# Softmax and head division over two banks of PSUM per operation, in a six-layer local-attention kernel

## The chip, the cores and the metric

The kernel runs on one core of one Trainium2 chip. The metric is the device time of one execution in microseconds. Five engines work side by side, each through its own queue in order: TensorE (PE) does matrix products and transposes, VectorE (DVE) and ScalarE (ACT) do elementwise work and reductions, GpSimd (POOL) does elementwise work on data in SBUF, and SyncE (SP) issues the transfers. They wait for each other on semaphores.

## The reference, cut to what matters

One time-mixing layer with a norm comes first, then six layers of local attention and a gated feed-forward over 2048 tokens of width 128, then a last norm. What the change touches is in the attention, with 16 heads of 64 and windows of 32 tokens that see themselves and the window before:

```
sim = jnp.einsum('bhwie,bhwje->bhwij', bq, bk2) * QK_SCALE
sim = jnp.where(mask, -jnp.finfo(sim.dtype).max, sim)
attn = jax.nn.softmax(sim, -1)
out = jnp.einsum('bhwij,bhwje->bhwie', attn, bv2)
...
for i in range(DEPTH):
    x = attn_layer(shift_tokens(x), Wqkv[i], q_scale[i], k_scale[i], Wo[i]) + x
    x = ffn_layer(shift_tokens(x), ln_g[i], ln_b[i], W1[i], b1[i], W2[i], b2[i]) + x
```

The feed-forward of a layer is a norm over the width, a product up to twice 341, a gelu on one half times the other, and a product down.

## The kernel before

The tokens are 16 tiles of 128, so six layers are 96 tiles in a row. The function `layers` runs steps s = -1 to 99. A step works on several tiles at once, each in a different phase: tile s + 1 is projected ("p": queries, keys, their squares, the inverse root of the sums, the unit vectors, the values), tile s has its queries and keys transposed and its scores made ("a"), tile s - 1 is mixed with the values, divided and sent through the output matrix ("b"). The feed-forward takes two tiles together: in an odd step the centred input and its variance ("norm") and the product down of an earlier pair ("down"), in an even step the normed input and the products up ("up"). Steps -1 to 6 and 95 to 99 are written out, 7 to 94 are a loop over pairs of an odd and an even step.

The order of the work on each engine is the order in which the functions are written. There is no scheduler. An engine that waits holds up all that is behind it in its queue.

PSUM holds four buffers of two banks, `proj_a`, `proj_b`, `att` and `turn` (in the functions `bank_a`, `bank_b`, `bank_s`, `bank_t`). The heads with an even number lie in the first bank, those with an odd number in the second. So each of the scores (in `turn`) and the mixed heads (in `att`) fills two banks, and the kernel before takes them bank by bank:

- `centre_scores(par)` on DVE: the row maxima of one bank (L1053, into `row_max`), then scores minus maximum (L1056, into `logits`).
- `weigh(par)` on ACT: the exponential of one bank (L949, into `probs`).
- `divide_out(par)` on DVE: mixed heads of one bank times the inverse of the mass (L1045, into `heads_out`).

PE makes the scores of both banks in one interleaved run (L1228) and so signals both at its end; the same holds for the mixed heads (L1202).

In an even step two operations of the feed-forward stand between the banks. On DVE `norm_n` (L1102), the centred input times the inverse deviation that PE's L1259 spread over the partitions, is between `centre_scores(0)` and `centre_scores(1)`. On ACT `normed` (L1009), `norm_n` with gain and bias, is between `weigh(0)` and `weigh(1)`. PE's products up (L1152) wait for `normed`, and stand in PE's queue behind the output product (L1265).

The other names that matter: `squares` (ACT L942) and their `sums` (DVE L1039); the inverse root, nine small operations on DVE (L88 to L104); `unit` (DVE L1064), first of the queries, then of the keys; on POOL `across` (L886), `along` (L920), `rotated` (L894), `turns` (L905), the shifted inputs `shift_f` and `shift_a` (L874, L875, L913, L914); PE's transposes (L1135), its query and key projections (L1168, L1183) and its value projection (L1240), which waits for `unit` of the queries.

Of the kernel before, what the change touches and what calls it, by code (L numbers as in the profile page):

```python
# [26 lines left out]
ALU = mybir.AluOpType  # L27
ACT = mybir.ActivationFunctionType
AX = mybir.AxisListType
# [4 lines left out]
HEADS, HEAD = 16, 64  # L34
PAIRS = HEADS // 2
INNER = HEADS * HEAD
DEPTH = 6
WINDOW = 32
# [27 lines left out]
def after(engine, semaphore, count):  # L66

    if not isinstance(count, int) or count > 0:
        engine.wait_ge(semaphore, count)
# [633 lines left out]
def layers(nc, ctx, given):  # L703
# [9 lines left out]
    bank_a, bank_b, bank_s, bank_t = (given[k] for k in ("proj_a", "proj_b", "att", "turn"))  # L713
    passed = given["passed"]

    with ExitStack() as own:
        def sb(name, shape, dtype=F32):
            return own.enter_context(nc.sbuf_tensor(name, shape, dtype))

        def sem(name):  # L720
            return ctx.enter_context(nc.semaphore(name))
# [19 lines left out]
        row_max = sb("row_max", [128, HEADS])  # L741
        logits = sb("logits", [128, 2, PAIRS, 2 * WINDOW])
        probs = sb("probs", [128, PAIRS, 2, 2 * WINDOW])
        mass = sb("mass", [128, HEADS])
        inv_mass = sb("inv_mass", [128, HEADS])
        p_t = sb("p_t", [128, PAIRS, TILE])
        heads_out = sb("heads_out", [128, PAIRS, 2, HEAD])
# [28 lines left out]
        scored, maxed, centred, weighed = sem("scored"), sem("maxed"), sem("centred"), sem("weighed")  # L776
        massed, mass_inverted = sem("massed"), sem("mass_inverted")
        p_turned, p_laid, mixed, scaled_out = sem("p_turned"), sem("p_laid"), sem("mixed"), sem("scaled_out")
# [37 lines left out]
        with nc.Block() as block:  # L816
# [118 lines left out]
            def _(act):  # L935
                def step(s, h, odd, live):
                    p, a, b, mine = s + 1, s, s - 1, 1 - odd
# [4 lines left out]
                        act.activation(squares[j][:, :, :], by_head((bank_a, bank_b)[j]), ACT.Square)\  # L942
                            .then_inc(squared[j], 1)

                    def weigh(par):
                        act.wait_ge(centred, 2 * a + par + 1)
                        after(act, p_turned, 2 * a)
                        after(act, massed, a)
                        act.activation(probs[:, :, par, :], logits[:, par, :, :], ACT.Exp).then_inc(weighed, 1)  # L949

                    if live["down"]:
                        act.wait_ge(down_in, (layer_of(s - 5) + 1) * 32)
# [48 lines left out]
                        act.copy(v_tok[mine][:, :, :, :], bank_a[:, :, :].rearrange("p a (h e) -> p a h e", e=HEAD))\  # L1001
                            .then_inc(v_laid, 1)
                    if live["a"]:
                        weigh(0)
                    if live["up"]:
                        act.wait_ge(scaled_f, h + 2)
                        act.wait_ge(up_in, (layer_of(s - 4) + 1) * 48)
                        after(act, widened, NC_ * (h + 1))
                        act.activation(normed[:, :], norm_n[:, :], ACT.Identity, bias=w_ffn[:, F_B:F_B + 1],  # L1009
                                       scale=w_ffn[:, F_G:F_G + 1]).then_inc(normed_f, 1)  # L1010
                    if live["a"]:
                        weigh(1)
                    if live["norm"]:
                        act.wait_ge(dev_made, h + 2)
                        after(act, scaled_f, h + 1)
# [2 lines left out]
                        act.activation(dev_sq[:, :], bank_b[:, 0, 0:TWO], ACT.Square).then_inc(dev_squared, 1)  # L1018

                run(act, step)  # L1020

            @block.vector
            def _(dve):
# [9 lines left out]
                def step(s, h, odd, live):  # L1033
                    p, a, b, mine = s + 1, s, s - 1, 1 - odd
# [3 lines left out]
                        after(dve, rooted, ROOT_OPS * p)  # L1038
                        dve.tensor_reduce(sums[:, j, :], squares[j][:, :, :], AX.X, ALU.add).then_inc(summed[j], 1)  # L1039

                    def divide_out(par):
                        dve.wait_ge(mixed, 2 * b + par + 1)
                        dve.wait_ge(mass_inverted, b + 1)
                        after(dve, o_turned, 2 * b)
                        dve.tensor_tensor(heads_out[:, :, par, :], bank_s[:, par, :].rearrange("p (a e) -> p a e", e=HEAD),  # L1045
                                          inv_mass[:, :].rearrange("p (a b) -> p a b", b=2)[:, :, par].unsqueeze(2)
                                          .broadcast_to([128, PAIRS, HEAD]), ALU.mult).then_inc(scaled_out, 1)

                    def centre_scores(par):
                        heads = slice(PAIRS * par, PAIRS * par + PAIRS)  # L1050
                        scores = bank_t[:, par, :].rearrange("p (a c) -> p a c", a=PAIRS)
                        dve.wait_ge(scored, 2 * a + par + 1)
                        dve.tensor_reduce(row_max[:, heads], scores, AX.X, ALU.max).then_inc(maxed, 1)  # L1053
                        dve.wait_ge(maxed, 2 * a + par + 1)
                        after(dve, weighed, 2 * a)
                        dve.tensor_tensor(logits[:, par, :, :], scores,  # L1056
                                          row_max[:, heads].unsqueeze(2).broadcast_to([128, PAIRS, 2 * WINDOW]),
                                          ALU.subtract).then_inc(centred, 1)

                    def unite(j):  # L1060
                        dve.wait_ge(rooted, ROOT_OPS * p + ROOT_OPS)
# [22 lines left out]
                        sum_squares(0)  # L1084
                        sum_squares(1)
                    if live["b"]:
                        divide_out(0)
                        divide_out(1)
                    if live["p"]:
                        dve.wait_ge(summed[0], p + 1)  # L1090
                        dve.wait_ge(summed[1], p + 1)
# [3 lines left out]
                        unite(0)  # L1095
                        unite(1)
                    if live["a"]:
                        centre_scores(0)
                    if live["up"]:
                        dve.wait_ge(rstd_spread, h + 2)  # L1100
                        after(dve, normed_f, h + 1)
                        dve.tensor_tensor(norm_n[:, :], dev[:, :], bank_s[:, 1, 0:TWO], ALU.mult).then_inc(scaled_f, 1)  # L1102
                    if live["a"]:
                        centre_scores(1)
                    if live["down"]:
                        dve.wait_ge(narrowed, h + 1)
                        dve.scalar_tensor_tensor(xa[:, columns(s - 5, 2)], bank_b[:, 1, 0:TWO], w_ffn[:, F_B2:F_B2 + 1],
# [10 lines left out]
                    if live["p"]:  # L1118
# [5 lines left out]
                                          ALU.mult).then_inc(alonged[1], 1)  # L1124

                run(dve, step)

            @block.tensor
# [311 lines left out]
```

## Time and profile before

| | |
|---|---|
| median of 3 runs | 2161.71 us (2158.82 to 2162.98) |
| the profiled execution | 2161.64 us |
| its span, first to last instruction | 2159.5 us |
| mean granted TensorE clock over the span | 0.919 |
| granted clock from 400 to 2100 us | 1.00 |
| busy PE, DVE, POOL, ACT | 1890.9, 1694.1, 1457.0, 1170.8 us |

The profile is of one execution. Its page gives the busy time of each engine and the costliest groups of instructions; the trace behind it can be asked for who waited for whom and for the instructions in order of time. PE's rows name matrix products, PEld their weight loads, which overlap the products. Times in the rows are in microseconds from the start of the span.

### The profile page before, as it was taken

The page shows a single profiled execution, that of the slowest core. Times are in us where ns is not written, and L with a number is a line of the kernel's source. Part 1 is how long each engine was busy: PE and PEld are TensorE (multiplying, and loading weights), DVE is VectorE, ACT ScalarE, POOL GpSimd, SP SyncE. Part 2 cuts the span into 40 slices and gives each one's busy share as a digit, 9 for nine tenths or more (in the row PEclk, how much of TensorE's full clock was granted, in tenths as well). Part 3 has the DMA queues.
Part 4 walks back from the last instruction along what each step waited for, and adds up shares of the span by engine and source line. Part 5 has one row for each costly group of instructions (what it writes and reads, how often), then busy time and mean ns, then how long its engine had stood idle before and what let it go on. Part 6 is the DMA issues. An engine that isn't in the chain of part 4 may idle for free. (4 is left out here: it accounts for less than half of the span.)

```text
span 2159.5 us, 87406 instructions
## 1 busy us (share of the span) xinstructions
PE 1890.9 (88%) x34160; PEld 1385.6 (64%) x34160; DVE 1694.1 (78%) x3442; ACT 1170.8 (54%) x2085; POOL 1457.0 (67%) x1150
## 2 busy tenths in 40 slices
PE   6776766899999999999999999999999999999995
PEld 4555543676666666666666676666666666666664
DVE  5777775888888888878788888888888878888874
ACT  1111113566656666666666666666666666656662
POOL 0000005888888887878787888888787878787871
PEclk6555557999999999999999999999999999999997
DMA  4000001222232222322222322223222223222220
GB/s 140 1 0 0 0 0 40 61 61 60 58 88 64 71 56 55 86 65 67 55 57 58 87 72 65 58 58 85 65 66 55 56 56 84 73 62 58 58 59 20
DMA packets 93565, 123.18 MB, mean 57 GB/s; under 512 B 27760, under 2 KB 41808, under 8 KB 93392
## 3 DMA queue, kind: packets, MB, share of 16 engines
q1 hardware_dynamic: 93232, 122.42, 22.5%
q8 instruction: 31, 0.51, 0.1%
q10 hardware_dynamic: 288, 0.13, 0.0%
q14 instruction: 14, 0.11, 0.0%
HBM read 20.74 MB, written 1.05 MB: 10 GB/s over the span
## 5 line engine op out<-in xcount | busy, mean ns | idle before, releaser
L886 POOL TENSOR_TENSOR across<-unit,turns 128x512 f32<-128x512 f32 x384 | 525.2, 1389 | 263.3 <-issue 252.3
L894 POOL TENSOR_TENSOR rotated<-along,across 128x1024 f32<-128x1024 f32 x192 | 496.2, 2584 | 20.4 <-POOL along L920 9.6
L1039 DVE TENSOR_REDUCE sums<-squares 128x16 f32<-128x1024 f32 x192 | 234.1, 1219 | 162.7 <-ACT squares L942 156.7
L1135 PE MATMUL turn<-identity,rotated 128*128 128x128 f32 x1536 | 204.2, 276 | 53.5 <-POOL rotated L894 53.5
L1135 PEld LDWEIGHTS turn<-identity,rotated 128*128 128x128 f32 x1536 | 172.1, 141 | 116.0 <-issue 101.1
L920 POOL TENSOR_TENSOR along<-unit,turns 128x1024 f32<-128x1024 f32 x96 | 227.6, 2371 | 0.0
L1240 PE MATMUL proj_a<-w_qkv,shift_a 128*128 128x512 f32 x384 | 189.5, 616 | 35.1 <-DVE unit L1064 25.4
L1001 ACT COPY val<-proj_a 128x1024 f32<-128x1024 f32 x96 | 97.2, 1012 | 179.6 <-PE proj_a L1240 179.6
L1265 PEld LDWEIGHTS att<-o_t,w_o 128*128 128x128 f32 x1536 | 188.2, 193 | 6.1 <-issue 1.0
L1168 PE MATMUL proj_a<-w_qkv,shift_a 128*128 128x512 f32 x384 | 185.7, 607 | 3.9 <-POOL shift_a L874 2.6
L1265 PE MATMUL att<-o_t,w_o 128*128 128x128 f32 x1536 | 188.6, 276 | 0.0
L977 ACT COPY k_t<-turn 128x512 f32<-128x512 f32 x192 | 103.1, 589 | 151.2 <-PE turn L1135 151.2
L1122 DVE TENSOR_TENSOR along<-unit,turns 128x1024 f32<-128x1024 f32 x96 | 183.6, 1913 | 0.0
L1183 PE MATMUL proj_b<-w_qkv,shift_a 128*128 128x512 f32 x384 | 181.5, 595 | 0.0
L942 ACT ACTIVATE squares<-proj_a 128x1024 f32<-128x1024 f32 x96 | 98.3, 1024 | 116.3 <-PE proj_a L1168 116.3
L1202 PE MATMUL att<-v_win,p_t 64*32 64x64 f32 x12288 | 154.0, 225 | 2.9 <-issue 2.1
L1228 PEld LDWEIGHTS turn<-k_t,q_t 64*32 64x32 f32 x12288 | 128.0, 105 | 41.0 <-issue 40.7
L962 ACT COPY p_t<-att 128x512 f32<-128x512 f32 x192 | 103.0, 589 | 88.9 <-PE att L1135 88.9
L1202 PEld LDWEIGHTS att<-v_win,p_t 64*32 64x32 f32 x12288 | 135.6, 105 | 21.8 <-issue 19.2
L1045 DVE TENSOR_TENSOR heads_out<-att,inv_mass 128x512 f32<-128x512 f32 x192 | 123.6, 686 | 31.9 <-PE att L1202 31.7
L1228 PE MATMUL turn<-k_t,q_t 64*32 64x64 f32 x12288 | 143.9, 225 | 0.0
L1056 DVE TENSOR_TENSOR logits<-turn,row_max 128x512 f32<-128x512 f32 x192 | 132.8, 691 | 6.6
(183 smaller groups left out, 3783.2 us busy)
## 6 DMA issues: line engine op xcount, KB each, us to landing
v_win<-val SPq DMA_DIRECT2D x1536, 64.0 KB
w_qkv<-wqkv_dram SPq DMA_DIRECT2D x18, 512.0 KB, 3.9
w_o<-wo_dram SPq DMA_DIRECT2D x6, 512.0 KB, 4.3
where<-positions_dram SPq DMA_DIRECT2D x1, 2048.0 KB, 10.8
w_ffn<-ffn_dram SPq DMA_DIRECT2D x12, 170.5 KB, 2.3
w_ffn<-ffn_dram SPq DMA_DIRECT2D x6, 192.0 KB, 2.3
x_tok<-x_dram SPq DMA_DIRECT2D x4, 256.0 KB, 4.5
out_dram<-final SPq DMA_DIRECT2D x4, 256.0 KB, 2.4
```

Of the source, the lines that this page charges most:

```text
L886: pool.tensor_tensor(a[:, :, 1 - half, :], u[:, :, half, :], table, ALU.mult)\
L894: pool.tensor_tensor(rotated[j][:, :, :], along[j][:, :, :], across[j][:, :, :], ALU.add).then_inc(rotated_in[j], 1)
L920: pool.tensor_tensor(along[0][:, :, :], unit[0][:, :, :], turns[mine][:, 0, :].unsqueeze(1).broadcast_to([128, HEADS, HEAD]), ALU.mult).th ...
L1039: dve.tensor_reduce(sums[:, j, :], squares[j][:, :, :], AX.X, ALU.add).then_inc(summed[j], 1)
L1122: dve.tensor_tensor(along[1][:, :, :], unit[1][:, :, :], turns[mine][:, 2, :].unsqueeze(1).broadcast_to([128, HEADS, HEAD]), ALU.mult).the ...
L1135: mm = pe.transpose(bank[:, TILE * (i % 4):TILE * (i % 4) + TILE], buffer[:, TILE * i:TILE * i + TILE], identity[:, :])
L1168: mm = pe.matmul(bank_a[:, half, :], shift_a[mine][:, :], w_qkv[:, 512 * half:512 * half + 512], start=True, stop=True)
L1183: mm = pe.matmul(bank_b[:, half, :], shift_a[mine][:, :], w_qkv[:, base:base + 512], start=True, stop=True)
L1202: mm = pe.matmul(bank_s[WINDOW * w:WINDOW * w + WINDOW, par, HEAD * a_:HEAD * a_ + HEAD], p_t[rows, a_, WINDOW * w:WINDOW * w + WINDOW], v ...
L1228: mm = pe.matmul(bank_t[WINDOW * w:WINDOW * w + WINDOW, par, HEAD * a_:HEAD * a_ + HEAD], q_t[rows, a_, WINDOW * w:WINDOW * w + WINDOW], k ...
L1240: pe.matmul(bank_a[:, par, :].rearrange("p (a e) -> p a e", a=PAIRS), shift_a[mine][:, :], values[:, par, :, :], start=True, stop=True).th ...
L1265: mm = pe.matmul(bank_s[:, 0, 0:TILE], w_o[:, a_, :], o_t[:, a_, :], start=(a_ == 0), stop=(a_ == PAIRS - 1))
```

## The change

Each pair of operations becomes one that runs over both banks: maxima, subtraction, exponential and division. The semaphores are counted up by 2 in one go, so that the engines that wait need no change. In the even steps the feed-forward operations that stood between the banks now stand behind the single operations.

```diff
-                    def weigh(par):
-                        act.wait_ge(centred, 2 * a + par + 1)
+                    def weigh():
+                        act.wait_ge(centred, 2 * a + 2)
                         after(act, p_turned, 2 * a)
                         after(act, massed, a)
-                        act.activation(probs[:, :, par, :], logits[:, par, :, :], ACT.Exp).then_inc(weighed, 1)
+                        act.activation(probs[:, :, :, :].rearrange("p a b c -> p b a c"), logits[:, :, :, :], ACT.Exp)\
+                            .then_inc(weighed, 2)
...
                     if live["a"]:
-                        weigh(0)
+                        weigh()
                     if live["up"]:
...
-                    if live["a"]:
-                        weigh(1)
...
-                    def divide_out(par):
-                        dve.wait_ge(mixed, 2 * b + par + 1)
+                    def divide_out():
+                        dve.wait_ge(mixed, 2 * b + 2)
...
-                        dve.tensor_tensor(heads_out[:, :, par, :], bank_s[:, par, :].rearrange("p (a e) -> p a e", e=HEAD),
-                                          inv_mass[:, :].rearrange("p (a b) -> p a b", b=2)[:, :, par].unsqueeze(2)
-                                          .broadcast_to([128, PAIRS, HEAD]), ALU.mult).then_inc(scaled_out, 1)
...
+                        dve.tensor_tensor(heads_out[:, :, :, :].rearrange("p a b e -> p b a e"),
+                                          bank_s[:, :, :].rearrange("p b (a e) -> p b a e", e=HEAD),
+                                          inv_mass[:, :].rearrange("p (a b) -> p b a", b=2).unsqueeze(3)
+                                          .broadcast_to([128, 2, PAIRS, HEAD]), ALU.mult).then_inc(scaled_out, 2)
+
+                    def centre_scores():
+                        scores = bank_t[:, :, :].rearrange("p b (a c) -> p (b a) c", c=2 * WINDOW)
+                        dve.wait_ge(scored, 2 * a + 2)
+                        dve.tensor_reduce(row_max[:, :], scores, AX.X, ALU.max).then_inc(maxed, 2)
+                        dve.wait_ge(maxed, 2 * a + 2)
                         after(dve, weighed, 2 * a)
...
+                        dve.tensor_tensor(logits[:, :, :, :].rearrange("p b a c -> p (b a) c"), scores,
+                                          row_max[:, :].unsqueeze(2).broadcast_to([128, HEADS, 2 * WINDOW]),
+                                          ALU.subtract).then_inc(centred, 2)
...
                     if live["a"]:
-                        centre_scores(0)
+                        centre_scores()
                     if live["up"]:
                         dve.wait_ge(rstd_spread, h + 2)
                         after(dve, normed_f, h + 1)
                         dve.tensor_tensor(norm_n[:, :], dev[:, :], bank_s[:, 1, 0:TWO], ALU.mult).then_inc(scaled_f, 1)
-                    if live["a"]:
-                        centre_scores(1)
```

On DVE, at the end of an even step (step 6), the queue reads before:

```order
L1064 TENSOR_TENSOR unit<-proj_b,inv_norm 128x1024 [waits k_acrossed,k_alonged,rooted]
L1053 TENSOR_REDUCE row_max<-turn 128x8 [waits scored]
L1056 TENSOR_TENSOR logits<-turn,row_max 128x512 [waits weighed,maxed]
L1102 TENSOR_TENSOR norm_n<-dev,att 128x256 [waits normed_f,rstd_spread]
L1053 TENSOR_REDUCE row_max<-turn 128x8 [waits scored]
L1056 TENSOR_TENSOR logits<-turn,row_max 128x512 [waits weighed,maxed]
L1111 TENSOR_TENSOR xb<-att,xa 128x128 [waits attended]
```

and now:

```order
L1063 TENSOR_TENSOR unit<-proj_b,inv_norm 128x1024 [waits k_acrossed,k_alonged,rooted]
L1052 TENSOR_REDUCE row_max<-turn 128x16 [waits scored]
L1055 TENSOR_TENSOR logits<-turn,row_max 128x1024 [waits weighed,maxed]
L1100 TENSOR_TENSOR norm_n<-dev,att 128x256 [waits normed_f,rstd_spread]
L1107 TENSOR_TENSOR xb<-att,xa 128x128 [waits attended]
```

`norm_n` has both banks of scores ahead of it in place of one.

On ACT, at the end of the same even step, the queue reads before:

```order
L992 COPY o_t<-att 128x512 [waits attended,o_turned] x2
L996 ACTIVATE k_t<-k_t,carry_scale 128x8x32 [waits scored]
L1001 COPY val<-proj_a 128x1024 [waits v_spread,v_projected]
L949 ACTIVATE probs<-logits 128x8x64 [waits massed,p_turned,centred]
L1009 ACTIVATE normed<-norm_n,w_ffn 128x256 [waits widened,up_in,scaled_f]
L949 ACTIVATE probs<-logits 128x8x64 [waits massed,p_turned,centred]
```

and now:

```order
L993 COPY o_t<-att 128x512 [waits attended,o_turned] x2
L997 ACTIVATE k_t<-k_t,carry_scale 128x8x32 [waits scored]
L1002 COPY val<-proj_a 128x1024 [waits v_spread,v_projected]
L949 ACTIVATE probs<-logits 128x2x8x64 [waits p_turned,massed,centred]
L1010 ACTIVATE normed<-norm_n,w_ffn 128x256 [waits widened,up_in,scaled_f]
```

`normed` now has the whole exponential ahead of it, and that waits for the whole subtraction.

## Rows read from the trace of the kernel before

**Rows 1.** The page's first part: busy us (share of span) x instructions, by engine.
```profile
PE 1890.9 (88%) x34160; PEld 1385.6 (64%) x34160; DVE 1694.1 (78%) x3442; ACT 1170.8 (54%) x2085; POOL 1457.0 (67%) x1150
```
**Rows 2.** Who waited for whom: us in total, times, longest us.
```profile
DVE sums L1039 <- ACT squares L942: 156.7, 146, 7.5
...
ACT squares L942 <- PE proj_a L1168: 116.3, 96, 6.1
...
PE turn L1135 <- POOL rotated L894: 53.5, 51, 2.2
...
PE att L1135 <- DVE heads_out L1045: 24.0, 47, 1.3
...
PEld proj_b L1152 <- ACT normed L1009: 7.5, 44, 0.2
```
**Rows 3.** Timeline, end of an even step: start us, us, engine, line, operation [idle before <-releaser].
```profile
1019.99 0.68 DVE L1053 TENSOR_REDUCE row_max<-turn 128x8 f32<-128x512 f32 x1
...
1020.84 0.59 PE L1259 MATMUL att<-rstd_diag,ones 128*128 128x256 f32 x2
...
1021.27 1.95 PE L1265 MATMUL att<-o_t,w_o 128*128 128x128 f32 x16
1021.47 0.42 DVE L1102 TENSOR_TENSOR norm_n<-dev,att 128x256 f32<-128x256 f32 x1
...
1021.80 0.69 DVE L1053 TENSOR_REDUCE row_max<-turn 128x8 f32<-128x512 f32 x1
1022.02 0.63 ACT L949 ACTIVATE probs<-logits 128x512 f32<-128x512 f32 x1
...
1022.52 0.69 DVE L1056 TENSOR_TENSOR logits<-turn,row_max 128x512 f32<-128x512 f32 x1
1022.55 0.59 ACT L1009 ACTIVATE normed<-norm_n,w_ffn 128x256 f32<-128x256 f32 x1
...
1023.20 1.99 PE L1152 MATMUL proj_b<-normed,w_ffn 128*128 128x256 f32 x8
```
**Rows 4.** Timeline, the odd step after it, from the division of the heads.
```profile
1032.95 1.29 DVE L1045 TENSOR_TENSOR heads_out<-att,inv_mass 128x512 f32<-128x512 f32 x2 [0.28 <-PE att L1202]
...
1034.54 0.29 POOL L874 COPY shift_a<-xa 64x128 f32 x1 [0.38 <-POOL shift_f L914]
1034.60 0.27 DVE L92 TENSOR_TENSOR root_work<-inv_norm 128x32 f32<-128x32 f32 x1
1034.88 0.29 POOL L875 COPY shift_a<-xa 64x128 f32 x1
1034.90 0.32 DVE L94 TENSOR_TENSOR root_work<-root_work,sums_min 128x32 f32<-128x32 f32 x1
...
1035.93 0.19 DVE L102 TENSOR_TENSOR root_work<-root_work,sums_min 128x32 f32<-128x32 f32 x1
...
1037.80 0.67 PE L1240 MATMUL proj_a<-w_qkv,shift_a 128*128 128x512 f32 x1 [0.57 <-DVE unit L1064]
...
1037.84 1.27 POOL L886 TENSOR_TENSOR across<-unit,turns 128x512 f32<-128x512 f32 x1 [2.66 <-issue]
```
**Rows 5.** Durations: one line's (ns min/median/max), then groups of the page (mean ns).
```profile
L1064 DVE TENSOR_TENSOR unit<-proj_a,inv_norm x96: 1223/1225/1226, 341.6 to 2086.4; 128x1024 f32<-128x1024 f32 x96
...
L1039 DVE TENSOR_REDUCE sums<-squares 128x16 f32<-128x1024 f32 x192 | 234.1, 1219 | 162.7 <-ACT squares L942 156.7
...
L1001 ACT COPY val<-proj_a 128x1024 f32<-128x1024 f32 x96 | 97.2, 1012 | 179.6 <-PE proj_a L1240 179.6
...
L992 ACT COPY o_t<-att 128x512 f32<-128x512 f32 x192 | 102.3, 587 | 6.7 <-PE att L1135 6.7
```
**Rows 6.** Timeline: POOL's last product and PE's transposes of it, even step, then odd.
```profile
1014.92 1.09 PE L1135 MATMUL turn<-identity,rotated 128*128 128x128 f32 x8 [1.00 <-POOL rotated L894]
...
1029.78 2.38 POOL L894 TENSOR_TENSOR rotated<-along,across 128x1024 f32<-128x1024 f32 x1
...
1032.66 1.09 PE L1135 MATMUL turn<-identity,rotated 128*128 128x128 f32 x8
```

More of the change, by code:

```diff
@@ L1049, in centre_scores @@
[L1049 to L1054, printed above, removed]
+                        dve.tensor_tensor(heads_out[:, :, :, :].rearrange("p a b e -> p b a e"),
+                                          bank_s[:, :, :].rearrange("p b (a e) -> p b a e", e=HEAD),
+                                          inv_mass[:, :].rearrange("p (a b) -> p b a", b=2).unsqueeze(3)
+                                          .broadcast_to([128, 2, PAIRS, HEAD]), ALU.mult).then_inc(scaled_out, 2)
@@ L1055, in centre_scores @@
+                    def centre_scores():
[3 more added lines that the diff above has]
+                        dve.wait_ge(maxed, 2 * a + 2)
                         after(dve, weighed, 2 * a)
-                        dve.tensor_tensor(logits[:, par, :, :], scores,
-                                          row_max[:, heads].unsqueeze(2).broadcast_to([128, PAIRS, 2 * WINDOW]),
-                                          ALU.subtract).then_inc(centred, 1)
+                        dve.tensor_tensor(logits[:, :, :, :].rearrange("p b a c -> p (b a) c"), scores,
+                                          row_max[:, :].unsqueeze(2).broadcast_to([128, HEADS, 2 * WINDOW]),
+                                          ALU.subtract).then_inc(centred, 2)
@@ L1086, in step @@
                     if live["b"]:
-                        divide_out(0)
-                        divide_out(1)
+                        divide_out()
                     if live["p"]:
```

## The prediction

> **What bounds the kernel now.** The layers' first `unit` starts at 341.6 us [rows 5], and they fill the rest but for the last norm. Their 96 steps repeat in pairs, an odd step and an even one. Which end is last inside such a pair has to be read from the order of time, since no engine is full: the page gives PE 88% of the span and DVE 78% [rows 1]. I read first who waited for whom, and then one pair in the timeline.
>
> The waits [rows 2] show PE as the engine that rarely stops. It stops in the even steps for the last product of the rotation on POOL (53.5 us, 51 times), and in the odd steps for the divided heads on DVE (24.0 us, 47 times). Its weight loads stop 44 times for `normed`, but only for 7.5 us in all. DVE in contrast waits for ACT's squares for 156.7 us, and those squares wait for a projection on PE. So DVE is mostly behind PE and not ahead of it, and a microsecond saved on DVE is worth something only in front of an instruction for which PE, or the POOL chain, is waiting.
>
> The even step's end [rows 3]: PE runs the 1.95 us of L1265 from 1021.27 to 1023.22 and goes on at 1023.20 with L1152, which needs `normed`. `normed` ran on ACT from 1022.55 to 1023.14. There is **no slack**: `normed` is finished when PE is. It comes from `norm_n` on DVE, which ran at 1021.47, straight after the first bank's subtraction and as soon as PE's L1259 (1020.84 + 0.59 = 1021.43) had its operand. The second bank's maximum and subtraction came after it, at 1021.80 and 1022.52.
>
> The odd step [rows 4]: once PE has the heads mixed, DVE divides both banks (1.29 us for two operations that overlap a little), runs the nine small operations of the inverse root, and makes the unit vectors, for which PE then waits 0.57 us at L1240 (1037.80). The POOL chain that the next even step waits for begins there as well. Two of the small operations, L92 and L94, took 0.27 and 0.32 us where L102, the same kind and size, took 0.19; in that stretch POOL copies `shift_a` (1034.54 to 1035.17).
>
> The even step's stall for POOL is 1.00 us at 1014.92, and in the odd step POOL had its `rotated` at 1029.78 + 2.38 = 1032.16, 0.50 us before PE took it at 1032.66 [rows 6].
>
> **The change, part by part.** First the durations. A DVE product from PSUM over both banks is already in the trace: `unit` 128x1024 takes 1.225 us. A reduce of 1024 takes 1.219. On ACT a 1024-wide copy takes 1.012 and a 512-wide copy 0.587, so 512 more elements cost 0.425; the exponential of one bank takes 0.63, and both in one 1.06 [rows 3, 5]. The ends for the exponential: 1.02, as the 1024-wide squares or copy take, and 1.26, twice the 0.63. For the DVE operations: 1.22 and 1.37 (twice 0.69). I take the low ones for DVE, since a row of just that form has them.
>
> (a) Maximum and subtraction in the **odd** steps. Four operations of 0.68 or 0.69, 2.74 us, become two of 1.22 with a gap of 0.03 (as 1021.80 + 0.69 to 1022.52 [rows 3]), 2.47. What comes next on DVE there is the feed-forward residual `xa` and then `xb`, which waits for PE's L1265, and PE asks for the probabilities only in its next step. Worth nothing.
>
> (b) The same in the **even** steps, where `norm_n` stood between the banks. Now it is behind both. The maximum runs 1019.99 to 1021.21, the subtraction from 1021.24 to 1022.46, and `norm_n` after that, not at 1021.47. Nor can ACT start `normed` at once, since the exponential of both banks is ahead of it in ACT's queue: it waits for the whole subtraction (the first bank's waited only for a quarter of the work), runs 1022.49 to 1023.55, and `normed` starts about 0.10 before that ends, as it did before (1022.55 against 1022.65): 1023.45. Before: 1022.55. That is **+0.90 us**, and PE had no slack [rows 3]. `norm_n` itself is done by 1022.9 and so is not the last. PE stands still for some 0.9 us in front of L1152.
>
> (c) What the delay carries along. In the odd step that follows everything on PE queues behind L1152, and ACT, then DVE, wait for PE there [rows 2]. Only POOL is not delayed. In an odd step it had 0.50 us to spare, now it has more, so it takes back nothing. The even step's 1.00 us of waiting for POOL can't absorb it either: that POOL chain starts from `unit` of the odd step, behind the delay. So the +0.90 enters whole.
>
> (d) `heads_out` in one operation: 1.29 becomes 1.22, **-0.07 us** in front of the root in the odd step, on the path. In the even step PE waits for POOL then, and it is worth nothing.
>
> (e) A side effect: POOL's copies of `shift_a` stay where they are, while DVE's L92 and L94 come 0.83 later, at about 1035.43, after their end at 1035.17 [rows 4]. If the overlap was what made them long, both fall to 0.19: (0.27 - 0.19) + (0.32 - 0.19) = **-0.21 us** on the path. Bounds: 0 and -0.21. I take it whole, for every other small operation of the chain that met no POOL work took 0.19.
> The Trainium skill (SBUF — State Buffer, "Who interferes with whom") says that a DVE instruction with two SBUF inputs contends with a GpSimd instruction that reads SBUF; by this rule the gain of (e) is real, and by a reading in which the overlap is chance the sum would be 9.7 us longer. The trace agrees so far: L92 and L94 have two such inputs, and were long just there.
>
> Sum: there are 46 even steps that have both attention and the up-projection (steps 4 to 94). 46 x (0.90 - 0.07 - 0.21) = 46 x 0.62 = **+28.5 us**. The profiled execution took 2161.64 (span 2159.5), which is the median of the runs as well (2161.71). Forecast: 2161.6 + 28.5 = **2190 us**.
>
> **The rivals.**
> *No relief on the small operations.* As forecast, but (e) is 0: 46 x 0.83 = 38, so 2200 us. For it: L92 and L94 may be long for a reason that moves with them. Chance 0.17.
> *The wide operations cost twice the narrow ones.* Each bank of PSUM might be worked off as its own pass: maximum 1.36, subtraction 1.38, exponential 1.26. Then `normed` starts 1019.99 + 1.36 + 0.03 + 1.38 + 0.03 + 1.26 - 0.10 = 1023.95, 1.40 us late; the divide costs 0.08 more (twice 0.69 against 1.29); 46 x (1.40 + 0.08 - 0.21) = 58, so 2220 us. The rows of 1024 elements speak against it. Chance 0.05.
> *POOL is the clock of the pair.* If the POOL chain ran free of PE, PE's 1.00 us wait in the even step would shrink by the 0.90 and no more would be seen: 2158 to 2162 us, no change. It decides if the POOL chain starts before the delayed work. Against it: it starts with `unit`, and the engine idles 2.66 us before that [rows 4]. Chance 0.06.
> *DVE is the bound after all.* Then every step saves what DVE saves: 2.74 - 2.47 = 0.27 for the scores and 0.07 for the heads, 0.34 x 96 = 33 us: 2129 us, faster. For it: DVE works in the pair as much as any but PE. Against it: it is idle before the sums of the squares, 146 times in 192 [rows 2]. Half such a saving, where (b) turns out to be covered, ends near 2145. The point from which it decides: PE would need 0.90 us of slack in front of L1152, and it has none. Chance 0.07.
> The Trainium skill (VectorE: DVE Perf Modes, "The TRN2 errata") speaks for this rival: a fixed latency is paid per instruction, so fewer and larger tiles are to be preferred. The trace agrees on the fixed part (two of 0.69 against one of 1.225), but here it is paid where nobody waits.
> *The change does not do what it says* can be left out: the order of instructions shows the single wide operations.
>
> **How the numbers follow.** Forecast 0.65, no relief 0.17, twice as dear 0.05, POOL clock 0.06, DVE bound 0.07. Low end: in (b) the exponential at 1.02 and 0.2 us more absorbed per pair by some wait that I did not see, 46 x (0.62 - 0.04 - 0.20) = 17, rounded down to 2177. High end: no relief and the exponential at 1.26, 46 x (0.90 + 0.20 - 0.07) = 47: 2209, rounded up to 2210. These ends hold the first two cases, some 0.8. Faster by over 0.2% (what a measurement of this kernel can tell from no change): 0.07. Within 0.2%: 0.06. Slower: 0.87.
>
> **What would show it.** In the profile after: `norm_n` starts just behind the wide subtraction; `normed` some 0.9 us later relative to L1265's start (1.28 us behind it before, 2.2 after); PE idle before L1152 for about 0.9 us in 46 steps, released by ACT `normed`, some 40 us in all; L92 and L94 shorter on average; PE's wait for POOL in the even step still near 1.0; a pair some 0.62 us longer. It would be wrong if PE's wait in front of L1152 were small, if the wait for POOL shrank by what the other grew, or if the wide exponential took far from 1.06.

## The result

The changed kernel takes 2197.07 us (median of 4 runs, 2194.91 to 2198.16) against 2162.35 us before (median of 4 runs): slower, ratio 1.0163 with a 95% interval of 1.0145 to 1.018. That is 34.7 us more, where 28.5 had been forecast. The profiled execution's span is 2196.4 us, 36.9 more than before. Two executions below ran at a lower granted clock, 2426.44 us (0.73) among the ten of e1 and 2659.06 us (0.634) among the fifteen of the kernel before beside e1 to e4: the medians count them, the ratios leave them out.

The first part of the page and the group of the products up, of the changed kernel. The columns are those of [rows 1] and of the page's groups (busy us, mean ns | idle before, releaser):

```profile
PE 1891.4 (86%) x34160; PEld 1385.2 (63%) x34160; DVE 1663.8 (76%) x3154; ACT 1165.8 (53%) x1989; POOL 1455.2 (66%) x1150
...
L1148 PE MATMUL proj_b<-normed,w_ffn 128*128 128x256 f32 x384 | 97.6, 398 | 45.8 <-ACT normed L1010 45.8
```

DVE works 30 us less (1663.8 against 1694.1) and ACT 5 us less, and the kernel is 35 us longer. PE does the same work. What is new is in the last row: PE now stands 45.8 us in front of L1148 (L1152 before), all of it for `normed`. The waits answer to [rows 2]:

```profile
DVE sums L1038 <- ACT squares L942: 181.4, 152, 5.6
...
ACT squares L942 <- PE proj_a L1164: 114.4, 96, 6.1
...
PE turn L1131 <- POOL rotated L894: 53.7, 50, 3.8
...
PEld proj_b L1148 <- ACT normed L1010: 53.1, 45, 1.2
PE proj_b L1148 <- ACT normed L1010: 45.8, 46, 1.2
...
PE att L1131 <- DVE heads_out L1044: 20.1, 47, 1.4
```

The wait for `normed` appears in exactly 46 steps. The wait for POOL is the same as before (53.7 against 53.5): it has absorbed nothing. Most of what DVE saved turned up as waiting for ACT's squares (181.4 against 156.7), which are behind PE.

The end of an even step in the timeline, to be laid beside [rows 3]:

```profile
1035.25 1.22 DVE L1052 TENSOR_REDUCE row_max<-turn 128x16 f32<-128x1024 f32 x1
...
1036.53 1.95 PE L1261 MATMUL att<-o_t,w_o 128*128 128x128 f32 x16
1036.56 1.22 DVE L1055 TENSOR_TENSOR logits<-turn,row_max 128x1024 f32<-128x1024 f32 x1
...
1037.70 0.41 DVE L1100 TENSOR_TENSOR norm_n<-dev,att 128x256 f32<-128x256 f32 x1
1037.86 1.06 ACT L949 ACTIVATE probs<-logits 128x1024 f32<-128x1024 f32 x1 [0.48 <-DVE logits L1055]
...
1038.83 0.58 ACT L1010 ACTIVATE normed<-norm_n,w_ffn 128x256 f32<-128x256 f32 x1
...
1039.46 1.78 PE L1148 MATMUL proj_b<-normed,w_ffn 128*128 128x256 f32 x7 [0.99 <-ACT normed L1010]
```

`normed` starts 1038.83 - 1036.53 = 2.30 us behind PE's output product; before it was 1.28. PE idles 0.99 us.

The odd step, to be laid beside [rows 4]:

```profile
1009.72 1.61 PE L1198 MATMUL att<-v_win,p_t 64*32 64x64 f32 x128
...
1011.62 1.22 DVE L1044 TENSOR_TENSOR heads_out<-att,inv_mass 128x1024 f32<-128x1024 f32 x1 [0.39 <-PE att L1198]
...
1012.05 0.29 POOL L874 COPY shift_a<-xa 64x128 f32 x1 [0.38 <-POOL shift_f L914]
1012.40 0.29 POOL L875 COPY shift_a<-xa 64x128 f32 x1
1012.76 0.18 DVE L88 SCALAR_TENSOR_TENSOR sums_min<-sums 128x32 f32<-128x32 f32 x1
...
1013.21 0.19 DVE L92 TENSOR_TENSOR root_work<-inv_norm 128x32 f32<-128x32 f32 x1
1013.43 0.19 DVE L94 TENSOR_TENSOR root_work<-root_work,sums_min 128x32 f32<-128x32 f32 x1
...
1014.89 1.23 DVE L1063 TENSOR_TENSOR unit<-proj_a,inv_norm 128x1024 f32<-128x1024 f32 x1
```

POOL's copies are over at 1012.69 and L92 and L94 take 0.19 each. From L88 to `unit` it is 2.13 us. The same stretch before:

```profile
1031.16 1.56 PE L1202 MATMUL att<-v_win,p_t 64*32 64x64 f32 x128
...
1034.16 0.18 DVE L88 SCALAR_TENSOR_TENSOR sums_min<-sums 128x32 f32<-128x32 f32 x1
...
1036.47 1.23 DVE L1064 TENSOR_TENSOR unit<-proj_a,inv_norm 128x1024 f32<-128x1024 f32 x1
```

That was 2.31. From the end of the mixing to L88 it is 1012.76 - 1011.33 = 1.43 now and 1034.16 - 1032.72 = 1.44 before. By these rows a pair is longer by 1.00 (PE's gap, 0.99 against an overlap of 0.02) - 0.01 - 0.18 = 0.81 us, and 46 of them are 37 us, the difference of the spans.

That this meets the spans is in part chance, for the odd step shown is not the common one. The next one after it is:

```profile
1047.43 1.50 PE L1198 MATMUL att<-v_win,p_t 64*32 64x64 f32 x128
...
1049.05 1.23 DVE L1044 TENSOR_TENSOR heads_out<-att,inv_mass 128x1024 f32<-128x1024 f32 x1
...
1050.11 0.29 POOL L875 COPY shift_a<-xa 64x128 f32 x1
...
1050.19 0.25 DVE L88 SCALAR_TENSOR_TENSOR sums_min<-sums 128x32 f32<-128x32 f32 x1
...
1052.38 1.23 DVE L1063 TENSOR_TENSOR unit<-proj_a,inv_norm 128x1024 f32<-128x1024 f32 x1
```

The division starts 1.62 us behind the first product of the mixing, not 1.90, and L88 now meets POOL's second copy and takes 0.25. Averages over the pairs between 480 and 2080 us (42 before, 41 after), each from one `normed` to the next, give 36.85 us before and 37.58 after, **0.73 more**:

| part of the pair, us | before | after | difference |
|---|---|---|---|
| start of the output product to start of the products up | 1.93 | 2.92 | +1.00 |
| first product of the mixing to the division, odd step | 1.77 | 1.71 | -0.06 |
| start of the division to L88 | 1.21 | 1.14 | -0.06 |
| L88 to `unit` | 2.32 | 2.16 | -0.16 |
| the rest | | | +0.02 |

46 x 0.73 = 34 us, close to the 34.7 between the medians. The other 3 us of the spans lie outside these pairs: one early pair of the profiled execution took 39.6 us, where the twelve other traces have 36.7 to 37.4.

### The profile page after: what moved, and what is told of

It reads as the page before. It is cut to its first block and busy times, and to the rows that moved or that the text cites. A ratio compares the mean times of both kernels' runs of the same rounds, so it can differ in the third digit from the quotient of the medians.

```text
span 2196.4 us, 86892 instructions
## 1 busy us (share of the span) xinstructions
PE 1891.4 (86%) x34160; PEld 1385.2 (63%) x34160; DVE 1663.8 (76%) x3154; ACT 1165.8 (53%) x1989; POOL 1455.2 (66%) x1150
## 5 line engine op out<-in xcount | busy, mean ns | idle before, releaser
L1038 DVE TENSOR_REDUCE sums<-squares 128x16 f32<-128x1024 f32 x192 | 234.2, 1220 | 186.6 <-ACT squares L942 181.4
L1131 PE MATMUL turn<-identity,rotated 128*128 128x128 f32 x1536 | 205.0, 276 | 53.8 <-POOL rotated L894 53.7
L1044 DVE TENSOR_TENSOR heads_out<-att,inv_mass 128x1024 f32<-128x1024 f32 x96 | 117.6, 1225 | 33.6 <-PE att L1198 29.7
L1148 PE MATMUL proj_b<-normed,w_ffn 128*128 128x256 f32 x384 | 97.6, 398 | 45.8 <-ACT normed L1010 45.8
```

What stands on the lines that cost most here:

```text
L1131: mm = pe.transpose(bank[:, TILE * (i % 4):TILE * (i % 4) + TILE], buffer[:, TILE * i:TILE * i + TILE], identity[:, :])
```

## The experiments

The times in the table are medians, each beside runs of the kernel before on the same chip. The ratio is the one on record and need not be the quotient of the two medians.

| kernel | us | before, same chip | ratio and 95% interval |
|---|---|---|---|
| even steps bank by bank (e1) | 2165.74 | 2162.81 | 1.0005 (0.9993 to 1.0018) |
| place alone (e2) | 2186.06 | 2162.81 | 1.0115 (1.0095 to 1.0134) |
| feed-forward operations ahead (e3) | 2154.05 | 2162.81 | 0.9964 (0.9951 to 0.9976) |
| semaphores by 1 (e4) | 2190.04 | 2162.81 | 1.0127 (1.011 to 1.0144) |
| more POOL copies (e5) | 2195.98 | 2162.98 | 1.016 (1.0141 to 1.018) |
| division alone (e6) | 2164.46 | 2162.98 | 1.0003 (0.9987 to 1.0018) |
| late POOL copies (e7) | 2153.78 | 2162.98 | 0.9957 (0.994 to 0.9974) |
| e3 and e7 together (e8) | 2149.05 | 2162.98 | 0.9941 (0.9921 to 0.996) |
| POOL copies, shifted (e9) | 2199.28 | 2162.94 | 1.0165 (1.0145 to 1.0186) |
| e8 with semaphores by 1 (e10) | 2148.87 | 2162.94 | 0.9916 (0.9888 to 0.9945) |
| one semaphore by 4 (e11) | 2197.22 | 2162.94 | 1.0156 (1.0137 to 1.0176) |

### Is it the even steps (e1)?

```diff
                     if live["a"]:
-                        weigh()
+                        if live["up"]:
+                            weigh_one(0)
+                        else:
+                            weigh()
...
                     if live["a"]:
-                        centre_scores()
+                        if live["up"]:
+                            centre_one(0)
+                        else:
+                            centre_scores()
```

with `centre_one(1)` behind `norm_n` and `weigh_one(1)` behind `normed`, as before the change.

> The changed kernel, but in the even steps with an up-projection the maxima, subtraction and exponential are again one bank at a time with the feed-forward operations between the banks; everything else stays wide. My theory (the whole loss is the late `normed` of the even steps): back to the kernel before, 2162 us within 4, and PE's wait for ACT `normed` back from 45.8 us to under 3. Rival (the wide operations cost by themselves, wherever they stand): half of the loss or more stays, 2178 us or more.

The ratio is 1.0005, no change that can be measured. PE's waits are back:

```profile
L1175 PE MATMUL proj_b<-normed,w_ffn 128*128 128x256 f32 x384 | 97.4, 397 | 1.2 <-ACT normed L1019 1.2
L1175 PEld LDWEIGHTS proj_b<-normed,w_ffn 128*128 128x128 f32 x384 | 70.1, 192 | 17.2 <-ACT normed L1019 7.5 <-issue 1.7
```

The whole loss is in the even steps. The wide operations of the odd steps and the wide division together are worth nothing that can be measured, nor do they cost.

### Place or width (e2, e4)?

e2 is the kernel before with nothing but the place changed:

```diff
                         centre_scores(0)
+                        centre_scores(1)
                     if live["up"]:
...
-                    if live["a"]:
-                        centre_scores(1)
```

and the same for `weigh` on ACT.

> The kernel before, all operations one bank at a time, with nothing changed but the place: `norm_n` behind the second bank's subtraction, `normed` behind the second bank's exponential. Theory (place, not width): `normed` starts at 1021.80 + 1.42 (second maximum and subtraction, 0.33 us earlier without `norm_n` between) and one exponential later, some 0.9 us later than before, and L92 and L94 lose their overlap with POOL as in the changed kernel: 46 x (0.90 - 0.20) = 32, so 2194 us. Rival (width costs): near 2162 us.

2186.06 us: two thirds of the loss without one wide operation. My number was 8 us too high, and the trace shows the term: the second subtraction came earlier than I had it, since `norm_n` between the banks had itself waited for PE (it started 0.76 us behind the first subtraction's start, where the second maximum now starts 0.60 behind it).

```profile
1029.17 0.68 DVE L1052 TENSOR_REDUCE row_max<-turn 128x8 f32<-128x512 f32 x1
...
1031.21 0.69 DVE L1055 TENSOR_TENSOR logits<-turn,row_max 128x512 f32<-128x512 f32 x1
...
1032.48 0.60 ACT L1010 ACTIVATE normed<-norm_n,w_ffn 128x256 f32<-128x256 f32 x1
...
1033.13 1.13 PE L1150 MATMUL proj_b<-normed,w_ffn 128*128 128x256 f32 x4 [0.73 <-ACT normed L1010]
```

The second subtraction starts 2.04 us behind the first maximum, against 1022.52 - 1019.99 = 2.53 before [rows 3]. So 0.49 us are gained and not 0.33, and PE waits 0.73.

The trace of e2 shows one thing more. The bank-by-bank division starts 1.67 us behind the first product of the mixing on average, against 1.77 before. So the mixed heads come some 0.1 us sooner with the place alone, wide or not; why is open.

e4 looked at what the wide version adds to that. In the changed kernel the wide subtraction starts 0.09 us after the maximum ends (1035.25 + 1.215 to 1036.56), where 0.03 stood before. Over all steps it is 0.090 against 0.035, and 0.083 against 0.034 from the subtraction to the exponential where ACT was idle.

```diff
-                        dve.tensor_reduce(row_max[:, :], scores, AX.X, ALU.max).then_inc(maxed, 2)
-                        dve.wait_ge(maxed, 2 * a + 2)
+                        dve.tensor_reduce(row_max[:, :], scores, AX.X, ALU.max).then_inc(maxed, 1)
+                        dve.wait_ge(maxed, a + 1)
```

and the same for `centred`, `weighed` and `scaled_out`.

> The changed kernel with semaphores raised by 1 and not by 2 by each wide operation, the waits counted to match. In the changed kernel the gaps between maximum and subtraction and between subtraction and exponential are 0.085 us, where 0.03 to 0.04 stood before. Theory A (the step of 2 is what takes longer): gaps back to 0.03 to 0.04, the even step shorter by some 0.1 us and the odd by 0.05, 46 x 0.15 = 7 us, so 2190 us. Theory B (the gap comes with the wide operation or with the wait itself): gaps stay 0.085, 2197 us.

```profile
1031.47 1.22 DVE L1052 TENSOR_REDUCE row_max<-turn 128x16 f32<-128x1024 f32 x1
...
1032.72 1.23 DVE L1055 TENSOR_TENSOR logits<-turn,row_max 128x1024 f32<-128x1024 f32 x1
...
1033.98 1.06 ACT L949 ACTIVATE probs<-logits 128x1024 f32<-128x1024 f32 x1 [0.37 <-DVE logits L1055]
...
1035.58 1.78 PE L1148 MATMUL proj_b<-normed,w_ffn 128*128 128x256 f32 x7 [0.89 <-ACT normed L1010]
```

Theory A held for the gaps: they are 0.03 and 0.04 again, PE waits 0.89 instead of 0.99, and the time is 2190.04 us, as written down. The expected 0.05 of the odd step can't be seen: from the first product of its mixing to that of the even step it is 17.76 us on average with 1 and 17.74 with 2. A pair is 0.11 us shorter (37.58 to 37.47), 5 us for 46, so some 2 of the 7 us are not placed. Of the 35 us lost, the place makes up some 24 and the raising by 2 some 5 to 7. The rest is that `normed` stands behind one exponential of 1.06 us which needs the whole subtraction, and not behind two of 0.63, of which the first could start earlier: PE waits 0.89 here and 0.73 in e2, 46 x 0.16 = 7 us, where the medians of e4 and e2 are 4 apart.

### What does a raise by 4 cost (e11)?

```diff
-                        dve.tensor_reduce(row_max[:, :], scores, AX.X, ALU.max).then_inc(maxed, 2)
-                        dve.wait_ge(maxed, 2 * a + 2)
+                        dve.tensor_reduce(row_max[:, :], scores, AX.X, ALU.max).then_inc(maxed, 4)
+                        dve.wait_ge(maxed, 4 * a + 4)
```

> The changed kernel with the semaphore between the wide maximum and the wide subtraction raised by 4 and not by 2, its wait to match. e4 had 0.035 us there with 1, the changed kernel 0.085 with 2. Theory (each count more takes 0.05 us): 0.185 us with 4, on the path of the even step only, 46 x 0.10 = 5 us, 2202 us. Rival (anything but 1 costs one fixed 0.05): 0.085 and 2197 us.

2197.22 us, the rival. The gap is what it was with 2 (1032.43 + 1.215 to 1033.74 is 0.095):

```profile
1032.43 1.22 DVE L1052 TENSOR_REDUCE row_max<-turn 128x16 f32<-128x1024 f32 x1
1033.74 1.22 DVE L1055 TENSOR_TENSOR logits<-turn,row_max 128x1024 f32<-128x1024 f32 x1
```

So here, of the counts 1, 2 and 4, both that are not 1 cost the same.

### The wide division (e6)

```diff
-                        divide_out(0)
-                        divide_out(1)
+                        divide_out()
```

on the kernel before, with the changed kernel's `divide_out`.

> The kernel before with only the division of the heads in one wide operation. My sum had -0.07 us per pair for it, -3 us. In the changed kernel the wide division starts 0.11 us later behind PE's mixing (0.39 against 0.28 us of idle time), and from the end of the mixing to the root it is 1.43 against 1.44 us. So now expected: 0, 2162 us within 2. Against it: -3 us, 2159.

The ratio is 1.0003, nothing that can be measured. 0.07 us per pair would have been at the edge of what can be seen, so the runs alone don't prove it; the trace of e6 does. In its 42 odd steps the wide division reaches L88 in 1.14 us and not 1.21, the 0.06 that was forecast, but it starts 1.87 us behind the first product of the mixing and not 1.77. L88 then comes 0.03 later, `unit` at the same time, and the pair is 36.85 us as before.

### The small operations and POOL (e5, e7, e9)

e7 is the kernel before with one wait more, in POOL's queue ahead of the copies of `shift_a` in odd steps:

```diff
+                        if live["norm"] and live["p"]:
+                            pool.wait_ge(rooted, ROOT_OPS * p + ROOT_OPS)
                         shift_input(s + 2, odd, h - 4 if odd else h - 3)
```

> The kernel before with one wait more: in the odd steps POOL copies `shift_a` only once DVE's inverse root is done, while `unit` is made. It takes away the overlap of POOL with L92 and L94 and moves nothing else. Theory: L92 and L94 of odd steps at 0.19, 46 x 0.2 = 9 us less, 2153 us. Rival: no change, 2162; or slower, if the copies end so late that POOL starts `across` late.

2153.78 us, 9 less, as computed:

```profile
1032.92 0.19 DVE L92 TENSOR_TENSOR root_work<-inv_norm 128x32 f32<-128x32 f32 x1
1033.15 0.19 DVE L94 TENSOR_TENSOR root_work<-root_work,sums_min 128x32 f32<-128x32 f32 x1
...
1034.85 0.29 POOL L874 COPY shift_a<-xa 64x128 f32 x1 [2.35 <-DVE inv_norm L104]
```

It is this relief that the changed kernel had got by itself, but for 0.04 us: in 29 of the 41 odd steps between 480 and 2080 us L88 was lengthened by a copy, and its average over all 41 is 0.23 us, where e7 has 0.18. The Trainium skill (SBUF — State Buffer, "Who interferes with whom") says that a DVE instruction with two SBUF inputs contends with a GpSimd instruction that reads SBUF; taking the reads away took the delay away, which agrees.

The other way round was harder. e5 puts POOL work back under L92 and L94 in the changed kernel:

```diff
                         shift_input(s + 2, odd, h - 4 if odd else h - 3)
+                        if live["norm"] and live["p"]:
+                            pool.tensor_tensor(spare[:, 0, 0:32], ones[:, 0:32], ones[:, 32:64], ALU.mult)
+                            for k in range(1, 4):
+                                pool.tensor_copy(spare[0:64, k, :], ones[0:64, :])
```

> The changed kernel with extra work on POOL in the odd steps, behind the copies of `shift_a`, where POOL idles for 3.56 us: one small product and three copies of 64x128 into an unused buffer, so that POOL reads SBUF while DVE runs L92 and L94. Theory (those two are lengthened by POOL's reads): in odd steps L92 and L94 take 0.25 to 0.35 again and not 0.19, other operations of the root may lengthen too, 46 x 0.2 = 9 us, so 2206 us. Rival (the relief came from something else): they stay at 0.19 and the time at 2197 us.

My theory missed and the rival's numbers came: 2195.98 us, and both operations stayed at 0.19 although copies ran over them.

```profile
1012.81 0.28 POOL L920 TENSOR_TENSOR spare<-ones 128x32 f32<-128x32 f32 x1
1013.04 0.78 POOL L922 COPY spare<-ones 64x128 f32<-64x128 f32 x3
```

```profile
1013.24 0.19 DVE L92 TENSOR_TENSOR root_work<-inv_norm 128x32 f32<-128x32 f32 x1
1013.46 0.19 DVE L94 TENSOR_TENSOR root_work<-root_work,sums_min 128x32 f32<-128x32 f32 x1
```

e9 shifts them, by a product of 96 columns in place of 32.

> As e5, with POOL's small product 96 columns wide and not 32, so that the three extra copies start some 0.13 us later, at about 1013.17, 1013.43 and 1013.69 where L92 starts at 1013.24 and L94 at 1013.46. In e5 the copies ran over both without lengthening them, but each of them had started 0.13 to 0.20 us before the DVE operation; in the kernel before they had started 0.02 to 0.06 us before. Theory (a DVE operation with two SBUF inputs is held only when it starts right behind the start of a POOL copy): L92 and L94 of odd steps lengthen to about 0.3 again, the time grows by 46 x 0.15 to 0.2, 7 to 9 us over e5, 2203 to 2205 us. Rival (POOL's copies of this kind never hold DVE): both stay at 0.19, 2196 us.

```profile
1011.36 0.40 POOL L920 TENSOR_TENSOR spare<-ones 128x96 f32<-128x96 f32 x1
...
1011.54 0.27 DVE L90 SCALAR_TENSOR_TENSOR inv_norm<-sums_min,magic 128x32 int32<-128x32 int32 x1
1011.84 0.20 DVE L92 TENSOR_TENSOR root_work<-inv_norm 128x32 f32<-128x32 f32 x1
1012.08 0.20 DVE L94 TENSOR_TENSOR root_work<-root_work,sums_min 128x32 f32<-128x32 f32 x1
```

2199.28 us. Both guesses on record missed: the ratios of e9 and e5 (1.0165 and 1.016) can't be told apart, and L92 did lengthen, though not by the copies. In the step shown the product, longer now, held L90 for 0.08 us. In 30 of 41 odd steps it held L92 instead, which then took 0.27. The three copies lengthened nothing by more than 0.02.

What decides can be read from the traces. The rows above have it: L90 ends at 1011.81, the product at 1011.76; before the change [rows 4] L92 ended at 1034.87 and L94 at 1035.22, the copies that they had started in at 1034.83 and 1035.17. In the thirteen traces 2034 operations of the root (L88 to L104) took over 0.205 us. Each of them had started inside a POOL operation, and each ended 0.04 to 0.05 us behind that operation's end. An operation of 0.19 us is thus lengthened only if more than about 0.15 us of the POOL operation are left when it starts. The added copies take 0.29 us and each had run for about 0.13 or more when the DVE operation began, so they held next to nothing. An overlap in the rows does not by itself mean a delay, and what counts is how much of POOL's operation is still to come.

### The order that the profile asks for (e3, e8, e10)

e3 keeps every wide operation and turns the order round. On DVE `norm_n` goes between the wide maximum and the wide subtraction, on ACT `normed` goes ahead of the exponential:

```diff
                         dve.tensor_reduce(row_max[:, :], scores, AX.X, ALU.max).then_inc(maxed, 2)
+                        between()
                         dve.wait_ge(maxed, 2 * a + 2)
...
-                    if live["a"]:
-                        weigh()
                     if live["up"]:
                         act.wait_ge(scaled_f, h + 2)
...
+                    if live["a"]:
+                        weigh()
```

where `between` is `norm_n` in the steps that have it.

> The changed kernel with all operations wide, but `norm_n` on DVE between the wide maximum and the wide subtraction, and `normed` on ACT ahead of the wide exponential. Theory: `normed` comes at about 1022.0 on the clock of the trace before, earlier than PE's L1265 ends; the exponential is done some 0.9 us before PE asks for the probabilities. PE's wait for `normed` under 3 us in all, time 2161 us within 4. Rival: the wide operations make something else late (the exponential before the probabilities' transposes, the gelu behind the table load), 2170 us or more.

2154.05 us, 7 less than expected, which is outside my 4, and 43 less than the changed kernel.

```profile
1020.15 0.60 ACT L1008 ACTIVATE normed<-norm_n,w_ffn 128x256 f32<-128x256 f32 x1
1021.13 1.06 ACT L949 ACTIVATE probs<-logits 128x1024 f32<-128x1024 f32 x1 [0.37 <-DVE logits L1056]
```

```profile
1021.07 1.89 PE L1153 MATMUL proj_b<-normed,w_ffn 128*128 128x256 f32 x8
```

`normed` is done 0.3 us before PE asks. Where the 9 us against the kernel before come from, the average pair shows (36.66 us against 36.85). The products up start 0.14 us sooner behind the output product (1.78 against 1.93), since PE's first weight load no longer waits, and the first eight of them take 0.10 less (1.89 against 1.99 [rows 3]). L88 to `unit` is 0.06 shorter (2.26 against 2.32), as L92 and L94 are at 0.19 and L96 at 0.29. Against these, 0.11 more pass from the first product of the mixing to L88. Together 0.19 x 46 = 9 us.

e8 is e3 with e7's wait, e10 that with semaphores raised by 1.

> Both together: all operations wide, `norm_n` between the wide maximum and subtraction and `normed` ahead of the exponential, and the POOL copies of the odd steps behind the inverse root. Theory: the two are independent, 2161 - 9 = 2152 us, faster than both kernels. Rival: with DVE's work shorter the copies collide with something else, and it is no better than either alone.

2149.05 us, better than the 2152 expected. It is not the sum of both gains (8.8 + 9.2 = 18): e3 already had a part of e7's relief, and a pair of e8 is only 0.11 us shorter than one of e3 (36.55 against 36.66).

> As e8 (all wide, feed-forward operations ahead, late POOL copies), with semaphores raised by 1. On the path of an odd step that saves 0.05 us behind the mixing (the wait of PE's transposes for `heads_out`), nothing in the even step, where `normed` is early: 46 x 0.05 = 2 us, so 2147 us. It would be the fastest version. Rival: no difference from e8, 2149.

2148.87 us, no different from e8: the rival on record. The ratio of e10 is 0.9916, the interval reaching from 0.9888 to 0.9945: both beat the kernel before and the changed one, e10 by some 48 us over the latter, though the two come from different sets of runs.

## Why the prediction was right

**The bound and the place** were right. PE had no slack in front of the products up, and the 46 even steps pay; e1 puts the whole loss there.

**(a), the odd steps' scores, nothing:** right (e1).

**(b), +0.90 for the late `normed`:** the mechanism was right, the size 0.10 too small (+1.00 on average). The three wide durations were read well from rows of the same size: 1.215, 1.224 and 1.057 against 1.22, 1.22 and 1.06. What I mis-sized are the two gaps, taken as 0.03 each from signals of one count. With a raise by 2 each is 0.05 longer. With a raise by 1 (e4) PE waits 0.89. It had not occurred to me that the diff's `then_inc(..., 2)` was a part of the change.

**(c), nothing absorbs it:** right. The wait for POOL stayed at 53.7 us, and from `unit` of the odd step to the mixing of the even one both kernels take 12.72 us.

**(d), -0.07 for the wide division:** wrong, it is 0 (e6). The term counted the operation from its start to its end, and there it holds (1.14 us to L88 against 1.21). But the wide division starts later behind the mixing, by 0.10 us in e6. It waits for the second bank's signal where the first of two waited for the first bank's; both signals come at the very end of the mixing, so this alone need not be the reason, and the cause of the 0.10 stays open.

**(e), -0.21 for the small operations:** real, as e7 shows, but 0.16 on average. L92 and L94 did fall to 0.19 in every odd step between 480 and 2080 us; L88, which the sum did not look at, ran into the copies instead.

**A term that the sum did not have:** with `norm_n` and `normed` moved, the mixed heads come about 0.1 us sooner (e2). In the changed kernel it covers what (d) missed. That part of the agreement is luck.

The sum was 0.62 per pair and the average pair has 0.73: +0.10 in (b), +0.05 in (e), -0.06 in (d) and the missing term together, +0.02 in the rest. 46 x 0.11 = 5 of the 6 us by which the medians exceed the forecast.

**The rivals.** No relief (2200) lay 3 us from the measured time, but for the wrong reason: the relief was there, and other terms were larger. That the time alone would have picked this rival, and the rows of L92 and L94 reject it, is worth noting. POOL as the clock of the pair, and DVE as the bound, fell by the waits. The rule of the Trainium skill (VectorE: DVE Perf Modes, "The TRN2 errata"), fewer and larger operations because each pays a fixed latency, is stated there for operations that read SBUF; here the trace agrees for DVE's busy time, which fell by 30 us though the merged ones read PSUM, and not for the kernel's.

## What to carry to other kernels

When two operations are merged, look first at what stood between them in the queue, and who waits for that; here the merge pushed a feed-forward operation with no slack behind work that nobody needed for another microsecond. Merged and with the urgent operation put first the same kernel gained 0.4% (e3), so the fault was the order, not the width. That the width itself brings anything is not shown: no run puts the urgent operations first and leaves the others bank by bank. Time saved on an engine that waits for another one only shows up as a longer wait.

## What the runs showed that was not expected

A semaphore raised by 2 or by 4 reached its waiter about 0.05 us later than one raised by 1: the gap between a wide maximum and the subtraction that waits for it was 0.090 us with 2 (L1052 to L1055) and with 4 (e11), and 0.034 with 1 (e4), with the same operations. Such a signal lies on the path twice in each of 46 even steps, which is 5 us; the kernel with 1 was 7 us shorter.

POOL's two copies of 0.29 us cost DVE 0.2 us per pair, 9 us in all, only because of the moment at which they ran (e7). A small DVE operation that was lengthened by one ended 0.04 to 0.05 us behind the copy's end, in each of thirteen traces.
